# A three-stage decoder layer on one core: scatters ahead of GpSimd's splits, the last turn's sum in thirds, the tile map in four parts, and a tail shared between three engines

## The chip, the core and the metric

The kernel runs on one core of a Trainium2 chip. The time is the device time of one execution in microseconds, as the median of several runs. Five engines each work through their own queue in order: TensorE (PE), VectorE (DVE), ScalarE (ACT), GpSimd (POOL) and SyncE (SP, which here only issues DMAs). They wait for each other through semaphores.

## The reference

The input is 16 sequences of 56 tokens with 128 features, and for each sequence a context of 1500 rows with 96 features.

```
x = layernorm(x + mixer(x))                       # causal convolution, cumulative sums, gate
x = layernorm(x + attention(x, ctx))              # q = x Wq, k and v from the context, softmax over 1500
logits = x Wr + br; top two of 8 experts; w = softmax(top two)
o_e    = relu(x W1_e + b1_e) W2_e + b2_e          # 128 -> 512 -> 128
f = layernorm(x + sum over the two chosen experts of w_e o_e) * gamma + beta
x = layernorm(x + f)
```

## The kernel before

Two sequences make a pair of 112 rows, so there are eight pairs (0 to 7). The program has four stages.

1. The mixer, for two halves of the batch (0 to 75 us of the trace).
2. The attention loop. `attend_turn(i)` overlaps pairs: TensorE makes the scores of pair i+1, the context sum of pair i-1 and the transposes of pair i's weights in three thirds (`turn_weights`). VectorE finds the maximum of 1500 scores, copies two thirds of the transposed weights, and makes norms. ScalarE does the exponentials and the last third. `last_turn()` ends the loop for pairs 6 and 7.
3. The experts. Pairs 0 to 6 are routed: each row's two experts are found (`logits`, `top_two`, `select`), the row gets a slot in its expert's region (`ranks` on TensorE, `place` on VectorE), and GpSimd's indirect DMA `scatter(i, w)` writes it to HBM tensor `slots`; there are 14 such scatters. TensorE then works through a sequence of 28 items: five dense passes of pair 7 (all its rows through experts 0 to 4), 20 tiles of 128 routed rows, and three more dense passes. Item n is `hidden(n)` (16 matmuls) and `outs(n)` (13); ScalarE and VectorE split the hidden values into a high and a low half between them (`hidden_high`, `hidden_low`). Tiles 0 to 7 are the first tile of each expert; which experts own the other 12 is the tile map, found by 12 small VectorE operations on row totals. `turn_tile(t)` transposes a loaded tile; it waits for the load, and SyncE issues the loads only once all 14 scatters have landed (`r_scat`).
4. The tail. SyncE loads the two expert outputs of each row (`got`), TensorE adds them to x2 in PSUM for two pairs at a time (four quarters), and two layer norms follow before the store.

The order on each engine is the order of the code, written by hand. GpSimd's code is one list that mixes four jobs: `split_low` (half of an expert's weights, 128x512, which TensorE wants only in stage 3), `low_rows` and `second_weights` (which finish a row before its scatter), `plus_beta` (x2 + beta, wanted only in the tail) and `scatter`. `pause(k)` is a small memset that spaces scatters. The semaphores that matter are `r_slot` (slots found), `r_wt` and `r_row` (row complete), `a_et`, `a_et2` (transposed weights read), `r_map` (tile map found), `t_ld` (tile loaded), `f_y` (sums ready), `f_rstd`, `f_rstd2` (inverse deviations).

The lines that the prediction's steps touch:

```
1366 maximum       1416 slot_c in place    1433-1452 tile_map      1470 turned_copy (VectorE)
1750 scatter       1734 split_low          1730 plus_beta          931 turned_copy (ScalarE)
543 scores  553 turn_weights  566 context_sum  765-767 hidden  780-784 outs  744 turn_tile
806 summed (tail)  1668-1691 the two norms' moments  893-895 inverse deviation  1123 final_norm
```

## Time and profile before

| | |
|---|---|
| median of 3 runs | 206.45 us (205.98 to 206.97) |
| the profiled execution's own time | 205.7 us |
| its span in the trace | 203.9 us (1.8 us lie around it) |
| busy: TensorE matmul, VectorE, ScalarE, GpSimd | 173.8, 154.4, 117.6, 61.7 us |
| mean granted TensorE clock | 0.97 |

The trace lists instructions with their start, length and engine, and in brackets the idle time in front of an instruction and who ended it. The shares of busy time are means over stages: between 144 and 182 us TensorE is never idle, in the last 17 us it works for 3.9 us. "x48" on a TensorE row counts matmul records; an fp32 matmul leaves two.

### The profile page before, as it was taken

How to read it: one execution, taken by the hardware profiler on the slowest of the kernel's cores; microseconds unless marked ns; L12 is line 12 of the kernel's file. 1: busy time of each engine (PE TensorE's matmuls, PEld its weight loads, DVE VectorE, ACT ScalarE, POOL GpSimd, SP SyncE). 2: the span in 40 equal slices, each digit the busy share in tenths (PEclk: the TensorE clock that was granted, in tenths of full speed). 3: DMA queues.
4: the chain of work that ended last, by engine and by line, in shares of the span. 5: the costliest groups of instructions: out<-in, count | busy, mean ns of one | idle time of the engine just before them, and what ended most of it. 6: DMA issues, size and time to landing. Idle time of an engine off the chain costs nothing.

```text
span 203.9 us, 4768 instructions
## 1 busy us (share of the span) xinstructions
PE 173.8 (85%) x1721; PEld 127.5 (63%) x1721; DVE 154.4 (76%) x394; ACT 117.6 (58%) x246; POOL 61.7 (30%) x82
## 2 busy tenths in 40 slices
PE   7999999969799978799799998785999999996400
PEld 6554556644353664564656787584999999994300
DVE  1659999988979668558967885677688888743890
ACT  2189979722664515697676954442566777650544
POOL 4000000000040000029697568881045655550000
PEclk9999999999999999999999999997899999999965
DMA  6999999993899278779856911104234100005011
GB/s 133 335 212 294 229 296 259 407 412 140 217 351 323 81 253 208 270 187 309 208 200 189 345 47 36 35 25 106 57 83 104 40 22 26 19 0 161 2 45 45
DMA packets 13467, 34.20 MB, mean 168 GB/s; under 512 B 2096, under 2 KB 5606, under 8 KB 13443
## 3 DMA queue, kind: packets, MB, share of 16 engines
q1 hardware_dynamic: 12356, 32.27, 53.0%
q0 software_dynamic: 1088, 1.62, 2.6%
q8 instruction: 14, 0.23, 0.5%
q14 instruction: 9, 0.07, 0.1%
HBM read 28.01 MB, written 6.38 MB: 169 GB/s over the span
## 4 chain that ended last, share of the span: by engine, by line
PE 53%; DVE 20%; issue 10%; POOL 8%; ACT 4%; DMA 2%; POOLq 0%; ACTq 0%; DVEq 0%; SPq 0%
PE bank L490 9%; POOL ret L1832 8%; PE bank L543 8%; PE bank L566 6%; PE bank L509 5%; PE bank L500 5%; PE bank L553 5%; PE bank L478 4%; DVE neg_max L1366 2%; PE bank L767 2%; PE bank L784 2%; DVE ph L1470 2%; DMA ctxT_slot<-ret 1%; DVE xtok L1684 1%; PE bank L806 1%
## 5 line engine op out<-in xcount | busy, mean ns | idle before, releaser
L1084 ACT ACTIVATE ctx_slot<-bank 128x512 f16<-128x512 f32 (+1 forms) x28 | 16.3, 582 | 18.8 <-PE bank L767 18.7
L1832 POOL DMA_INDIRECT ret<-ctx_slot,ctxT_slot x20 | 19.7, 986 | 24.5 <-ACT ctx_slot L1097 20.8
L1598 DVE SCALAR_TENSOR_TENSOR ctx_slot<-bank,ctx_slot 128x512 f16<-128x512 f32 (+1 forms) x28 | 18.8, 671 | 9.6 <-ACT ctx_slot L1084 7.2
L543 PE MATMUL bank<-ctxT_slot,w_conv 97*64 97x500 f32 x96 | 21.8, 589 | 2.4 <-ACT pc L926 1.4
L1754 POOL TENSOR_TENSOR home<-home 128x896 f32<-128x896 f32 x1 | 2.1, 2077 | 55.3 <-ACT home L882 55.3
L490 PE MATMUL bank<-xpad,w_conv 128*128 128x448 f32 x48 | 18.5, 544 | 0.0
L784 PE MATMUL bank<-home,ctx_slot 128*112 128x128 f16 (+1 forms) x192 | 14.7, 227 | 3.2 <-DVE ctx_slot L1598 3.2
L1366 DVE TENSOR_REDUCE neg_max<-bank 120x1 f32<-120x1500 f32 x8 | 13.7, 1714 | 4.5 <-PE bank L543 4.5
L1734 POOL TENSOR_TENSOR home<-w_raw,home 128x512 f16<-128x512 f32 x10 | 11.5, 1164 | 14.8 <-DVE neg_max L1366 14.8
L1242 DVE TENSOR_TENSOR_SCAN home<-reset,home 128x896 f32<-128x896 f32 x8 | 15.8, 2008 | 0.0
L566 PE MATMUL bank<-ctx_slot,ph 125*64 125x96 f32 x336 | 15.4, 248 | 0.0
L784 PEld LDWEIGHTS bank<-home,ctx_slot 128*112 128x112 f16 (+1 forms) x192 | 12.6, 121 | 3.7 <-DVE ctx_slot L1598 3.5
L490 PEld LDWEIGHTS bank<-xpad,w_conv 128*128 128x128 f32 x48 | 9.1, 193 | 9.2 <-issue 8.7
L1750 POOL DMA_INDIRECT slots<-mix,slot_i x14 | 13.5, 963 | 4.6 <-issue 3.7
L566 PEld LDWEIGHTS bank<-ctx_slot,ph 125*64 125x64 f32 x336 | 14.1, 133 | 1.2 <-issue 0.7
L478 PE MATMUL bank<-reset 128*128 128x224 f32 x48 | 13.4, 424 | 1.4 <-DVE reset L1145 1.4
L543 PEld LDWEIGHTS bank<-ctxT_slot,w_conv 97*64 97x64 f32 x96 | 6.2, 133 | 13.0 <-issue 10.9
L765 PE MATMUL bank<-half_sb,b_hl 128*128 128x112 f16 (+1 forms) x64 | 13.8, 221 | 0.3 <-DVE turned_late L1561 0.3
L500 PE MATMUL bank<-home,w_blk 128*128 128x448 f32 x32 | 12.9, 545 | 0.0
L478 PEld LDWEIGHTS bank<-reset 128*128 128x128 f32 x48 | 10.7, 235 | 2.9 <-DVE reset L1145 1.4
L893 ACT ACTIVATE lnv<-mv,cst 112x2 f32<-112x2 f32 (+3 forms) x11 | 3.2, 293 | 15.6 <-DVE mv L1307 6.3
L767 PE MATMUL bank<-ctx_slot 128*128 128x128 f16 x144 | 12.0, 219 | 0.0
(223 smaller groups left out, 433.5 us busy)
## 6 DMA issues: line engine op xcount, KB each, us to landing
ctx_slot<-ctx SPq DMA_DIRECT2D x16, 576.0 KB, 5.7
ctxT_slot<-ctx_T SPq DMA_DIRECT2D x16, 562.5 KB, 9.5
w_raw<-w SPq DMA_DIRECT2D x16, 256.0 KB, 6.9
slots<-w_raw SPq DMA_DIRECT2D x4, 910.0 KB, 26.1
ctxT_slot<-slots SPq DMA_DIRECT2D x20, 65.0 KB, 1.9
convw_sb<-conv_w SPq DMA_DIRECT2D x3, 256.0 KB, 5.6
ctxT_slot<-ret SPq DMA_DIRECT2D x3, 224.0 KB, 3.1
small_sb<-small SPq DMA_DIRECT2D x1, 526.0 KB, 9.3
```

The lines of the kernel that those rows point to most:

```text
L478: mm = pe.matmul(bank[:, to, 0:HW // 2], reset[:, 0:D], reset[:, 0:HW // 2], start=True, stop=True)
L490: mm = pe.matmul(bank[:, Z[c, g], 0:HW], w_conv[:, g, k, :], xpad[:, HB * c:HB * (c + 1), k:k + L], start=(k == 0), stop=(k == TAPS - 1))
L500: mm = pe.matmul(bank[:, Y_BANK[c], 0:HW], w_blk[:, j, :], terms[:, j * HW:(j + 1) * HW], start=(j == 0), stop=(j == 2 * M - 1))
L543: mm = pe.matmul(bank[j * GAP:j * GAP + rows, n, 0:SN], qk_all[:, at:at + rows], ctxT_slot[:, s, j, n * SN:(n + 1) * SN], start=True, stop ...
L566: mm = pe.matmul(bank[j * GAP:j * GAP + rows, SUM_BANKS[i], 0:DC], expT_sb[i][:, c, j * GAP:j * GAP + rows], ctx_slot[0:KP, s, j, c, :], s ...
L767: mm = pe.matmul(to, w[:, 0, part, at], x[:, half, 0:cols], start=False, stop=(m == 2))
L784: mm = pe.matmul(to, h_[:, n % 3, f, 0:cols], w[:, 1, part, f * D:(f + 1) * D], start=False, stop=(h_ is hl and f == FC - 1))
L1084: nc.scalar.activation(hh[:, n % 3, :, 0:cols], bank[:, n % 3, :].rearrange("p (f t) -> p f t", f=FC) [:, :, 0:cols], ACT.Relu).then_inc(t ...
L1242: return V.tensor_tensor_scan(sums[:, w], reset[:, 0:W2], terms[:, w], 0.0, ALU.mult, ALU.add)
L1366: V.tensor_reduce(neg_max[0:GT, :], bank[0:GT, 0:SB, 0:SN], AX.XY, ALU.max, negate=True).then_inc(a_max, 1)
L1598: V.scalar_tensor_tensor(hl[:, n % 3, :, 0:cols], bank[:, n % 3, :].rearrange("p (f t) -> p f t", f=FC) [:, :, 0:cols], 0.0, hh[:, n % 3, ...
L1832: G.indirect_dma_start(ret[:], bass.IndirectOffsetOnAxis(ap=xs_u[:, t, D + 1:D + 2], axis=0), out_st[:, t % OB, :], None, bounds_check=2 * ...
```

## The change

- GpSimd: each `scatter` stands in front of the splits and of `plus_beta`; two of the six pauses go; the last three `plus_beta` move behind the scatters of output tiles 2, 3 and 4.
- The last turn: all three thirds of pair 7's weights are transposed before pair 6's context sum, pair 7's own sum is cut in three parts instead of two, and VectorE's and ScalarE's steps are put in another order. `ranks(4)` goes ahead of the first dense pass.
- Stage 3's start: pair 7's logits are read before its first low half; the tile map's 12 operations are spread over four places (`read_counts`, `count_extras`, `expert_of_tile`, `tile_map`); TensorE's first tile waits for `r_tot` (counts read) instead of `r_map`. The reads of the map into VectorE's registers begin four items later.
- The tail: pair 7, which needs nothing from the returned outputs, is normalised first, alone. For the others VectorE only centres and multiplies by gamma; ScalarE scales (`scaled`), TensorE adds x2 + beta in PSUM (`with_x2`), and the last norm is ScalarE's for quarters 0 and 1 and VectorE's for the rest. There are five stores instead of four.

The diff, cut to its core:

```diff
@@ tensor, turn_weights: @@
+                if third == 2 and i == PAIRS - 1:
+                    pe.wait_ge(a_et2, i)
@@ tensor, last_turn @@
                 turn_weights(q, 0)
                 turn_weights(q, 1)
+                turn_weights(q, 2)
                 context_sum(p)
                 turn_x2(p - 1)
                 ranks(2)
-                turn_weights(q, 2)
-                context_sum(q, range(0, KC // 2))
+                context_sum(q, range(0, KC // 3))
                 turn_sum(p)
                 logits(p - 1)
-                context_sum(q, range(KC // 2, KC))
+                context_sum(q, range(KC // 3, 2 * KC // 3))
                 values(p)
+                context_sum(q, range(2 * KC // 3, KC))
@@ tensor, turn_tile and the start of stage 3 @@
-                    pe.wait_ge(r_map, 1)
+                    pe.wait_ge(r_tot, 1)
...
+            ranks(4)
             hidden(0)
-            ranks(4)
+            logits(PAIRS - 1)
             totals()
...
-                if n == 0:
-                    logits(PAIRS - 1)
@@ tensor, tail @@
+            def returns(q):
+                w = slice(2 * q, min(2 * q + 2, XP))
+                added(SUM_AT[q], x2[:, w, :], start=True)
+                pe.wait_ge(g_ld[q], 16)
+                added(SUM_AT[q], got[:, w, 0, :])
+                added(SUM_AT[q], got[:, w, 1, :], stop=True).then_inc(f_y, 1)
+
+            def with_x2(q):
+                w = slice(2 * q, min(2 * q + 2, XP))
+                added(NORM_AT[q], x2b[:, w, :], start=True)
+                pe.wait_ge(f_scaled, q + 1)
+                added(NORM_AT[q], acc[:, w, :], stop=True).then_inc(f_sum, 1)
...
+            returns(0)
+            returns(1)
+            returns(2)
+            with_x2(0)
+            returns(3)
+            with_x2(1)
+            with_x2(2)
+            with_x2(3)
@@ scalar, end of the loop @@
+            turned_copy(PAIRS - 1)
             route_weights(2)
             high_rows(PAIRS - 3)
-            turned_copy(PAIRS - 1)
+            split_high(1, POOL_SPLITS - 1)
             turned_sum(PAIRS - 2)
             route_weights(3)
+            attended_inv_std(PAIRS - 2)
             turned_sum(PAIRS - 1)
-            attended_inv_std(PAIRS - 2)
+            high_rows(PAIRS - 2)
             attended_inv_std(PAIRS - 1)
-            high_rows(PAIRS - 2)
@@ scalar, tail @@
+            def scaled(q):
+                act.wait_ge(f_cent, q + 1)
+                act.wait_ge(f_rstd, q + 2)
+                for j in range(2 * q, min(2 * q + 2, XP)):
+                    ins = nc.scalar.activation(acc[:, j, :], acc[:, j, :], ACT.Copy, scale=rstd[:, j:j + 1])
+                ins.then_inc(f_scaled, 1)
@@ vector, last_turn @@
                 turned_copy(q)
+                select(2)
                 sum_copy(p)
...
+                attended_stats(p)
+                sum_copy(q)
                 select(3)
-                sum_copy(q)
-                attended_stats(p)
+                attended_norm(p)
                 place(3)
-                attended_norm(p)
-                attended_stats(q)
-                x2T_copy(p)
+                attended_stats(q, between=lambda: x2T_copy(p))
                 logit_read(p, q)
                 attended_norm(q)
                 top_two(p, q)
+                select(4)
                 dve.wait_ge(t_x7h, 1)
...
-                select(4)
                 place(4)
@@ vector, tail @@
+            def returned(q):
                 dve.wait_ge(f_y, q + 1)
+                moments(q + 1, returned_at, f_var)
+                dve.wait_ge(f_var, q + 2)
+                for j in range(2 * q, min(2 * q + 2, XP)):
+                    ins = V.scalar_tensor_tensor(acc[:, j, :], returned_at(j), mv[:, j, 0:1], par("gamma", PT),
+                                                 ALU.subtract, ALU.mult)
+                ins.then_inc(f_cent, 1)
+            def summed(q):
+                dve.wait_ge(f_sum, q + 1)
+                moments(q + 1, normed_at, f_var2)
@@ gpsimd: tile outputs @@
+                if 2 <= t < 5:
+                    plus_beta(PAIRS - 5 + t)
```

The first place is GpSimd's queue in the attention loop, from the low halves of the first rows on, before the change (L1725 `low_rows`, L1741 `second_weights`, L1730 `plus_beta`, L1734 `split_low`, L1750 `scatter`):

```order
L1725 TENSOR_TENSOR mix<-rows_late,mix 112x2x128 x2
L1741 TENSOR_TENSOR mix<-mix,tsm 112x2
L1730 TENSOR_TENSOR rows_late<-rows_late,small_sb 112x128 x2
L1734 TENSOR_TENSOR home<-w_raw,home 128x512
L1750 DMA slots<-mix,slot_i 7296x130
L1734 TENSOR_TENSOR home<-w_raw,home 128x512
L1750 DMA slots<-mix,slot_i 7296x130
L1725 TENSOR_TENSOR mix<-rows_late,mix 112x2x128
L1750 DMA slots<-mix,slot_i 7296x130
```

and after it (L1793, L1809, L1798, L1802 and L1818 are the same five):

```order
L1793 TENSOR_TENSOR mix<-rows_late,mix 112x2x128 x2
L1809 TENSOR_TENSOR mix<-mix,tsm 112x2
L1818 DMA slots<-mix,slot_i 7296x130
L1798 TENSOR_TENSOR rows_late<-rows_late,small_sb 112x128 x2
L1818 DMA slots<-mix,slot_i 7296x130
L1802 TENSOR_TENSOR home<-w_raw,home 128x512
L1818 DMA slots<-mix,slot_i 7296x130
L1802 TENSOR_TENSOR home<-w_raw,home 128x512
```

The first scatter now stands in front of two `plus_beta` and of every further split; later scatters move up in the same way.

The second place is VectorE's queue at the start of stage 3, before (L1598 `hidden_low`, L1378 to L1396 pair 7's logits and choice, L1580 to L1584 its weights):

```order
L1598 SCALAR_TENSOR_TENSOR ctx_slot<-bank,ctx_slot 128x4x112
L1378 TENSOR_TENSOR logit<-bank,small_sb 112x8
L1386 MAX top<-logit 112x8
L1388 TENSOR_TENSOR tsm<-top 112x1
L1390 MAX_INDEX topi<-top,logit 112x8
L1396 TENSOR_TENSOR chosen<-small_sb,topi 112x16
L1580 TENSOR_SCALAR rw<-chosen,tsm 112x8
L1581 TENSOR_SCALAR rw<-chosen,tsm 112x8
L1584 TENSOR_TENSOR rw<-rw 112x8
L1598 SCALAR_TENSOR_TENSOR ctx_slot<-bank,ctx_slot 128x4x112
L1625 SCALAR_TENSOR_TENSOR xtok<-bank,rw,rows_late 112x128
L1430 TENSOR_SCALAR counts<-bank 1x8
```

and after (L1640 is `hidden_low`, L1465 `read_counts`, L1622 to L1626 the weights, L1667 `pair_out`):

```order
L1414 TENSOR_TENSOR logit<-bank,small_sb 112x8
L1422 MAX top<-logit 112x8
L1424 TENSOR_TENSOR tsm<-top 112x1
L1426 MAX_INDEX topi<-top,logit 112x8
L1640 SCALAR_TENSOR_TENSOR ctx_slot<-bank,ctx_slot 128x4x112
L1432 TENSOR_TENSOR chosen<-small_sb,topi 112x16
L1465 TENSOR_SCALAR counts<-bank 1x8
L1622 TENSOR_SCALAR rw<-chosen,tsm 112x8
L1623 TENSOR_SCALAR rw<-chosen,tsm 112x8
L1626 TENSOR_TENSOR rw<-rw 112x8
L1640 SCALAR_TENSOR_TENSOR ctx_slot<-bank,ctx_slot 128x4x112
L1667 SCALAR_TENSOR_TENSOR xtok<-bank,rw,rows_late 112x128
```

Pair 7's logits stand in front of the first `hidden_low`, and of the tile map only one operation (L1465) is left before the second one. Before, all 12 followed pair 7's first output (L1625) in one run.

The third place is ScalarE's queue in the tail before, from its first instruction there (L893 and L895 an inverse deviation, L1123 a final norm):

```order
L893 ACTIVATE lnv<-mv,cst 112x2
L895 ACTIVATE rstd<-lnv 112x2
L893 ACTIVATE lnv<-mv,cst 112x2
L895 ACTIVATE rstd<-lnv 112x2
L893 ACTIVATE lnv<-mv,cst 112x2
L895 ACTIVATE rstd<-lnv 112x2
L893 ACTIVATE lnv<-mv,cst 112x2
L895 ACTIVATE rstd<-lnv 112x2
L1123 ACTIVATE x<-xtok,nmr,rstd 112x128 x2
L893 ACTIVATE lnv<-mv,cst 112x2
L895 ACTIVATE rstd<-lnv 112x2
```

and after, from the first inverse deviation of a quarter on (L916, L918; L1149 `scaled`, L1155 the final norm):

```order
L916 ACTIVATE lnv<-mv,cst 112x2
L918 ACTIVATE rstd<-lnv 112x2
L1149 ACTIVATE xtok<-xtok,rstd 112x128 x2
L916 ACTIVATE lnv<-mv,cst 112x2
L918 ACTIVATE rstd<-lnv 112x2
L1149 ACTIVATE xtok<-xtok,rstd 112x128 x2
L916 ACTIVATE lnv<-mv,cst 112x2
L918 ACTIVATE rstd<-lnv 112x2
L916 ACTIVATE lnv<-mv,cst 112x2
L918 ACTIVATE rstd<-lnv 112x2
L1149 ACTIVATE xtok<-xtok,rstd 112x128 x2
```

Between the inverse deviations ScalarE now also scales, and it reads its final norm from PSUM.

## Rows read from the trace of the kernel before

**Rows 1.** Part 4 of the page: the chain that ended last, by engine

```profile
PE 53%; DVE 20%; issue 10%; POOL 8%; ACT 4%; DMA 2%; POOLq 0%; ACTq 0%; DVEq 0%; SPq 0%
```

**Rows 2.** Busy time by stretch; its columns are in its first line

```profile
core 0: us, PE busy (x) PEld busy (x) DVE busy (x) ACT busy (x) POOL busy (x), PEclk, DMA share, GB/s
...
131.00:144.00 13.00, 9.76 (x150) 9.44 (x151) 8.99 (x35) 5.29 (x12) 6.33 (x11) 0.87 0.26 62
144.00:182.00 38.00, 38.00 (x686) 37.91 (x686) 29.88 (x62) 24.90 (x58) 19.25 (x20) 1.00 0.17 45
```

**Rows 3.** Timeline of VectorE, place(0) and place(1): start, length, engine, line, operation, idle

```profile
98.92 1.89 DVE L1416 TENSOR_TENSOR slot_c<-chosen,slot_e 112x32 f32<-112x32 f32 x1
...
115.12 0.20 DVE L1416 TENSOR_TENSOR slot_c<-chosen,slot_e 112x32 f32<-112x32 f32 x1
```

**Rows 4.** Timeline of GpSimd at the first scatter

```profile
98.87 0.77 POOL L1730 TENSOR_TENSOR rows_late<-rows_late,small_sb 112x128 f32<-112x128 f32 x2
99.60 1.16 POOL L1734 TENSOR_TENSOR home<-w_raw,home 128x512 f16<-128x512 f32 x1
102.06 1.12 POOL L1750 DMA_INDIRECT slots<-mix,slot_i  x1 [1.30 <-issue]
```

**Rows 5.** Timeline of TensorE, transposes of pairs 4 and 5

```profile
99.44 1.13 PE L553 MATMUL bank<-small_sb,pc 120*125 120x120 f32 x8
...
101.87 0.70 PE L553 MATMUL bank<-small_sb,pc 120*125 120x120 f32 x4 [0.16 <-DVE ph L1470]
...
107.86 1.13 PE L553 MATMUL bank<-small_sb,convw_sb 120*125 120x120 f32 x8
...
109.30 0.70 PE L553 MATMUL bank<-small_sb,convw_sb 120*125 120x120 f32 x4 [0.21 <-DVE ph L1470]
```

**Rows 6.** Timeline of GpSimd from the last splits to the last scatter

```profile
115.73 2.28 POOL L1734 TENSOR_TENSOR home<-w_raw,home 128x512 f16<-128x512 f32 x2
...
120.52 0.95 POOL L1750 DMA_INDIRECT slots<-mix,slot_i  x1 [0.15 <-POOL mix L1725]
...
136.16 0.95 POOL L1750 DMA_INDIRECT slots<-mix,slot_i  x1 [0.17 <-issue]
```

**Rows 7.** Timeline of SyncE's queue, loads of the first eight tiles

```profile
138.50 3.65 SPq L453 DMA_DIRECT2D ctxT_slot<-slots  x8
```

**Rows 8.** Part 6 of the page: count, KB each, median us from issue to landing

```profile
ctxT_slot<-slots SPq DMA_DIRECT2D x20, 65.0 KB, 1.9
```

**Rows 9.** Timeline of TensorE, its waits in the last turn and stage 3's start

```profile
122.65 1.21 PE L566 MATMUL bank<-ctx_slot,home 125*64 125x96 f32 x24 [0.65 <-ACT home L931]
...
136.41 0.43 PE L784 MATMUL bank<-home,ctx_slot 128*112 128x128 f16 x4 [0.83 <-DVE ctx_slot L1598]
...
140.54 0.68 PE L784 MATMUL bank<-home,ctx_slot 128*112 128x128 f16 x4 [2.41 <-DVE ctx_slot L1598]
```

**Rows 10.** Timeline of VectorE: x7's low half, pair 6's slots, tile map

```profile
130.53 0.27 DVE L1561 TENSOR_TENSOR turned_late<-bank,turned_late 128x112 f16<-128x112 f32 x1 [0.33 <-ACT turned_late L1074]
...
132.66 0.17 DVE L1419 TENSOR_REDUCE slot_i<-slot_c 112x2 int32<-112x16 f32 x1
...
137.33 0.61 DVE L1435 TENSOR_SCALAR counts<-counts 1x8 f32<-1x8 f32 x1
```

**Rows 11.** Timeline of the tail, VectorE and ScalarE

```profile
188.51 0.30 ACT L893 ACTIVATE lnv<-mv,cst 112x2 f32<-112x2 f32 x1 [5.30 <-DVE mv L1671]
...
190.95 0.49 DVE L1688 BATCH_NORM_STATS2 stat<-xtok 112x6 f32<-112x128 f32 x2
...
193.69 0.49 DVE L1688 BATCH_NORM_STATS2 stat<-xtok 112x6 f32<-112x128 f32 x2
...
200.01 0.28 ACT L893 ACTIVATE lnv<-mv,cst 112x2 f32<-112x2 f32 x1
...
200.32 0.20 ACT L895 ACTIVATE rstd<-lnv 112x2 f32<-112x2 f32 x1
...
200.75 0.88 ACT L1123 ACTIVATE x<-xtok,nmr,rstd 112x128 f32<-112x128 f32 x2 [0.23 <-DVE nmr L1698]
```

More of the change, by code:

```diff
@@ L464, in _ @@
                 sp_.dma_start(got[:, w], ret.rearrange("(p i w) d -> p i w d", p=PT, i=XP)[:, w]).then_inc(g_ld[q], 16)
-            for q in range(4):
-                sp_.wait_ge(f_out, q + 1)
-                w = slice(2 * q, 2 * q + 2)
+            for n, w in enumerate((slice(XP, PAIRS), slice(0, 2), slice(2, 4), slice(4, 6), slice(6, XP))):
+                if n in (1, 2):
+                    sp_.wait_ge(f_out, n)
+                else:
+                    sp_.wait_ge(f_outv, n - 1 if n else 1)
                 sp_.dma_start(out[:, w, :], x1[:, w, :]).then_inc(s_store, 16)
-            sp_.wait_ge(s_store, 16 * 4)
+            sp_.wait_ge(s_store, 16 * 5)
         @block.tensor
@@ L1479, in attended_stats @@
                 a = loop.mark(V.bn_stats(attend_stat[:, s], res[:, s]))
+                if between:
+                    between()
                 loop.need(a)
@@ L1643, in _ @@
                     pair_out(n)
-                if n == 0:
-                    tile_map()
+                if n == 1:
+                    scanned = count_extras()
+                if n == 2:
+                    summed_tiles = expert_of_tile(scanned)
+                if n == 3:
+                    tile_map(summed_tiles)
                 if 4 <= n < 10:
                     split_low(n % 2, POOL_SPLITS + (n - 4) // 2)
-                for k in range(n - 1, n) if 1 <= n <= EXTRA else ():
-                    expert_of_extra(k)
+                if 5 <= n < 5 + EXTRA:
+                    expert_of_extra(n - 5)
                 if n == HEAD + E - 3:
@@ L1653, in _, with moments @@
                     staged(n - (HEAD + E - 3))
-            def summed_at(j):
-                if j == XP:
-                    return acc[:, j, :]
-                return bank[0:PT, (3, 7, 0, 1)[j // 2], (j % 2) * D:(j % 2 + 1) * D]
+            def moments(n, at, done):
+                pairs = range(XP, PAIRS) if n == 0 else range(2 * n - 2, min(2 * n, XP))
+                for j in pairs:
+                    a = own.mark(V.bn_stats(stat[:, j, :], at(j)))
+                own.need(a)
+                for j in pairs:
+                    a = V.bn_aggr(mv[:, j, :], stat[:, j, :])
+                a.then_inc(done, 1)
@@ L1694, in final_bias, with vector_final @@
             def final_bias(q):
                 w = slice(2 * q, 2 * q + 2)
-                dve.wait_ge(f_rstd2, q + 1)
+                dve.wait_ge(f_rstd2, q + 2)
                 V.scalar_tensor_tensor(nmr[:, w], mv[:, w, 0], -1.0, rstd2[:, w], ALU.mult, ALU.mult).then_inc(f_bias, 1)
+            def vector_final(n):
+                dve.wait_ge(f_rstd2, n + 1)
+                for j in range(XP, PAIRS) if n == 0 else range(2 * n - 2, min(2 * n, XP)):
+                    ins = V.tensor_scalar(x1[:, j, :], normed_at(j) if n else acc[:, j, :], mv[:, j, 0:1],
+                                          rstd2[:, j:j + 1], ALU.subtract, ALU.mult)
+                ins.then_inc(f_outv, 1)
@@ L1799, in _ @@
             second_weights(1)
+            scatter(2, 0)
             plus_beta(3)
+            scatter(2, 1)
             split_low(0, 4)
+            scatter(3, 0)
+            low_rows(4)
+            plus_beta(4)
+            scatter(3, 1)
             split_low(1, 4)
-            low_rows(4)
-            scatter(2, 0)
-            plus_beta(4)
-            scatter(2, 1)
-            pause(0)
-            scatter(3, 0)
-            low_rows(5)
-            scatter(3, 1)
-            second_weights(2)
-            pause(1)
-            scatter(4, 0)
-            pause(2)
+            second_weights(2)
+            scatter(4, 0)
+            low_rows(5)
             scatter(4, 1)
             second_weights(3)
-            pause(3)
+            pause(0)
             scatter(5, 0)
+            pause(1)
+            scatter(5, 1)
             low_rows(6)
-            scatter(5, 1)
             second_weights(4)
-            pause(4)
             scatter(6, 0)
-            pause(5)
+            pause(2)
             scatter(6, 1)
-            for i in range(PAIRS - 3, PAIRS):
-                plus_beta(i)
             for t in range(TILES):
```

158 lines of the change are left out of this document (78 added, 80 removed).

## The prediction, made before the changed kernel ran

> **What bounds the kernel now.** I read the chain of waits first. It lies on TensorE for 53% and on VectorE for 20%, GpSimd having 8% [rows 1]; so a gain must come from TensorE's gaps or from a stage where it has little to do. The table by stretch shows which: from 144 to 182 us TensorE is busy 38.0 of 38.0 us at a granted clock of 1.00, while from 131 to 144 us it is busy for 9.8 of 13 us and the mean clock is 0.87 [rows 2]. Nothing in this change shortens the 38 us. What it can shorten is the attention loop where TensorE waits, the 13 us after it, and the tail. For these I read the timelines of the engines.
>
> **The loop (pair 4's turn).** VectorE's slot_c operation lasts 1.89 us, where the same form takes 0.20 us one group later [rows 3]. It starts at 98.92 and ends at 100.81; GpSimd is in two plus_beta and then in a split until 100.76 [rows 4]. VectorE's copies of the transposed weights queue behind it, and TensorE gets to its last third 2.43 us after its first (101.87 - 99.44), against 1.44 us a turn later [rows 5]. The difference is 0.99 us. After the change the scatter stands ahead of plus_beta and of the split, and the scatter waits for the slots; so GpSimd reads nothing while slot_c runs. Gain 1.0 us. Bounds: up to 1.2, and down to -0.5 if the two splits, moved some 3 us, fall on the norm of that turn instead.
>
> The Trainium skill (SBUF — State Buffer, "Who interferes with whom") says that a VectorE instruction with two SBUF inputs contends with a GpSimd instruction that reads SBUF, and that the later one fully blocks. By that rule the trace agrees: 1.89 us against 0.20, ending 0.05 us after the split.
>
> **The last turn.** Pair 7's last third is transposed before pair 6's context sum, so the 0.65 us in which TensorE waited for ScalarE's copy is covered by 2.1 us of sum [rows 9]. The new wait on a_et2 is for a copy of pair 6 that is over before it; behind it in the queue is only that sum. Part is given back, since pair 7's norm still hangs on VectorE and ScalarE in turn, and select(4) now stands in front of x7's low half (two operations, 0.4 us). I follow the queues and get x7's low half 0.4 us earlier than 130.53 [rows 10]. ranks(4), 0.3 us, lies before hidden(0) in a wait instead of behind it.
>
> **From the last turn to the first tile.** TensorE reaches the first tile's transposes 0.47 us into the row at 140.54, at 141.0. On the way it waits 0.83 and 2.41 us [rows 9]. The second is VectorE in 12 small tile-map operations, each waiting for the one before (one is 0.61 us for eight numbers [rows 10], while GpSimd runs its last three plus_beta); pair 2's low half stands behind them. In four parts, no part is longer than about 0.9 us, less than the 1.5 us of one item, and the low halves come in time. The last moment at which TensorE would be ready is then 141.0 - 0.83 - 2.41 - 0.4 - 0.3 - 0.3 (half-clock part of the last outs, and pair 7's waits) = 136.8 at the latest, 136.4 by the sum of its items.
>
> But the tile has to be there. Ten scatters take 136.16 - 120.52 = 15.6 us, 1.74 us each [rows 6]. GpSimd is late with them: it does two splits from 115.73 [rows 6], although pairs 2 and 3 had slots one short operation after the slot_c that ends at 115.32 [rows 3]; and pair 6's slots are ready at 132.83 [rows 10] while the last two scatters start at 134.67 and 136.16. Now the scatters of pair 2 start at 115.6; nine spacings of 1.74 and the two splits put between (2.3 us) give 133.6. Pair 6's slots come some 1.5 us earlier (0.4 from the turn, and ranks(4) is no longer behind 0.8 us of hidden(0) and its queue), at 131.3; from there 0.2, 1.5 and nothing else give 133.0. I take 133.2, 3.0 us earlier than 136.16. The loads of the tiles were issued at 138.50 [rows 7], 2.3 us behind the last scatter; now 135.5. A load lands after 1.9 us [rows 8]: 137.4. So the first tile starts at 137.4 and no longer at 141.0; TensorE waits there 0.6 to 1.0 us for data in place of 3.2 us for VectorE. That is 3.6; I take 3.4 us, since this long walk forgets hand-offs. Bounds: 0.6 us, if the last scatter does not move (138.50 + 1.9 = 140.4), and 4.2 us, if data never hold TensorE.
>
> **The clock.** 13 us at a mean of 0.87 [rows 2] miss 13 x 0.13 = 1.7 us of full clock: half clock (1.2 GHz instead of 2.4) for some 3.4 us. It falls in the wait of 2.41 us, the four matmuls behind it take 0.68 us, while after the wait of 0.83 us the same four take 0.43 [rows 9]. With a longest wait of about 1 us the level of 2.4 GHz holds. 0.2 us of it is counted above: gain 1.4 us. Bounds 0 and 1.5.
>
> **The tile stage.** Three plus_beta now lie among the scatters of tile outputs, and four more map reads on VectorE beside the staged copies. VectorE is busy for 29.9 of the 38.0 us [rows 2], so it has some 0.4 us to spare per tile of 1.73 us, and a two-input operation that meets a plus_beta (0.4 us) loses it. I take -0.4 us, bounds 0 and -1.6 (four tiles late by 0.4).
>
> **The tail.** VectorE sets it: the same step recurs after 2.74 us (190.95, 193.69), and ScalarE ends last at 200.75 + 0.88 = 201.6 [rows 11]. Pair 7 goes into the wait for the returned outputs, some six short operations on VectorE where ScalarE's own wait is 5.30 us long [rows 11]. For the others VectorE keeps per quarter the moments twice and one multiplication, about 2.0 us, 8.8 us with the last norms, so it would be through at 196.5. ScalarE becomes the bound. From 188.5 on it has 8 inverse deviations at 0.51 (0.31 to the second instruction and 0.20) and 11 activations at 0.44 (0.88 for two) [rows 11]: 4.1 + 4.8 = 8.9 us, so 197.4, with hand-offs 197.8. Behind it stand VectorE's last two norms, 0.9 us: 198.7, 2.9 us before 201.6. The stores now come three in 1.5 us from one queue; I give 0.4 us back. Gain 2.5 us, bounds 1.0 (TensorE's added sums at half clock and each in the chain) and 3.2.
>
> **The sum** is against the profiled execution itself, 205.7 us (span 203.9 and 1.8 around it): 1.0 + 3.4 + 1.4 - 0.4 + 2.5 = 7.9, so 197.8. The median of the runs, 206.45, lies 0.75 above that execution; on its scale the forecast is 198.5 us.
>
> **Rivals.**
> - The clock falls all the same. TensorE's wait for the first tile lies between the 0.83 us that did no harm and the 2.41 us that did. If it does, the 1.4 us stay: 199.9. For it: the pause in the middle may come on top of the short ones around it. Chance 0.18.
> - The scatters don't come earlier. Their gate is pair 6's choice, and row 120.52 only says that GpSimd was late early on; if the last one is 1.5 us later than I think, tile and clock suffer: 1.5 + 0.5, 200.5. Chance 0.14, of which 0.04 for the following. A scatter that starts while VectorE is in a copy could be held up. Against it: the one at 102.06 ran beside copies of pair 4 and took 1.12 us instead of 0.95 [rows 4, 6]. The Trainium skill (SBUF — State Buffer, "SBUF: two separate sides") has this as a trap: during a VectorE operation that uses both ports, GpSimd cannot write the descriptors of its DMA. By that rule scatters moved into VectorE's busy turns would lose what they gain.
> - The tail gives nothing, because hand-offs among three engines replace one queue: each quarter goes VectorE, ScalarE, TensorE, VectorE, ScalarE, VectorE. Then 201.0. Against it: four quarters are in flight at a time. Chance 0.10.
> - Almost everything fails together: within 0.5% of before. Chance 0.04.
> - Slower. The tile stage passes from TensorE to VectorE: hidden_low, a staged copy of 2048 columns and now a map read per tile stand in one queue, and with GpSimd's plus_beta each tile could take 2.2 us in place of 1.73. The other terms bring 8.3 us over 20 tiles, so it decides from 0.42 us per tile on; at 0.47 (9.4 us) it gives 1.1 us above before, 207.5. Against it: the map reads stood beside such copies for three tiles before, and the 38 us show no gap [rows 2]. Chance 0.04.
>
> **Numbers.** The forecast has 0.50. Its own range is 197.3 to 199.6. The range for 8 in 10 takes in the clock, the late scatters and most of a lost tail: 196.5 to 202.0; its lower end is 2.0 us under the forecast, about what data that never hold TensorE (0.8), a better tail (0.7) and no loss in the tile stage (0.4) would give. About 0.5% is what a measurement of this kernel can tell from no change. Faster by more than that: 0.50 + 0.18 + 0.14 + 0.10 = 0.92, same 0.04, slower 0.04.
>
> **What the profile after would show.** slot_c of the first group at 0.2 us, and 1.4 us between TensorE's two groups of transposes in that turn. The last scatter about 4 us earlier on the clock of the trace (1.0 of it from the loop), the first tile loads 2.3 us behind it, TensorE's wait in front of the first tile ended by that load and about 1 us long, no granted clock under 0.97 between 130 and 143. 28 items without a gap from there. In the tail ScalarE busiest, its queue over about 2.9 us sooner after the first sum. I am wrong if the first tile's wait is over 2 us, if the tile stage shows gaps, or if VectorE is still the last in the tail.

## The result and the profile after

Median of 4 runs: 200.17 us (198.75 to 201.02), against 206.21 us (205.93 to 206.97) of the kernel before on the same chip; ratio 0.971, 95% interval 0.967 to 0.975. The profiled execution took 200.14 us with a span of 198.3 us: 5.6 us less than the 203.9 us before, where the forecast had 7.9. Medians here and below are over all executions of a kernel, while ratios and their intervals leave out executions more than 1.5% above the kernel's fastest.

The busy time by stretch shows where the forecast missed. These are rows of the changed kernel; after the stretch stand its length, then TensorE, its weight loads, VectorE, ScalarE, GpSimd, the granted clock, the DMA share and GB/s.

```profile
125.00:130.00 5.00, 3.46 (x19) 2.76 (x19) 3.81 (x20) 1.90 (x8) 4.09 (x8) 0.71 0.12 35
130.00:137.40 7.40, 7.40 (x79) 7.26 (x78) 3.96 (x18) 2.56 (x8) 3.74 (x6) 0.50 0.10 27
137.40:142.00 4.60, 4.40 (x83) 4.25 (x81) 3.51 (x13) 3.19 (x6) 0.00 (x0) 1.00 0.52 118
142.00:180.00 38.00, 38.00 (x686) 37.79 (x684) 31.13 (x67) 24.87 (x57) 22.06 (x23) 1.00 0.17 45
```

From 130 to 137.4 us TensorE never waits, but it is granted 0.50: 1.2 instead of 2.4 GHz. Before, the granted clock fell only at 140.5 us and was back by 144 [rows 2, 9]. The 38 us of tiles are full as they were [rows 2]; one gap of 0.20 us lies just before them, at 141.55 us.

The timeline of TensorE says what it did as the clock fell (start, length, engine, line, operation, idle time in front and who ended it):

```profile
98.86 1.13 PE L560 MATMUL bank<-small_sb,pc 120*125 120x120 f32 x8
100.30 0.70 PE L560 MATMUL bank<-small_sb,pc 120*125 120x120 f32 x4 [0.21 <-DVE ph L1515]
...
121.16 0.34 PE L616 MATMUL bank<-sel,half_sb 112*112 112x8 f16 x4 [0.54 <-DVE sel L1441]
...
125.34 0.32 PE L585 MATMUL bank<-small_sb,u_sb 120*97 120x120 f32 x1 [0.59 <-DVE u_sb L1509]
126.24 0.39 PE L616 MATMUL bank<-sel,half_sb 112*112 112x8 f16 x5 [0.58 <-DVE sel L1441]
...
127.45 0.98 PE L483 MATMUL bank<-reset 128*128 128x224 f32 x2
...
139.64 0.28 PE L752 MATMUL bank<-half_sb,ctxT_slot 128*128 128x128 f16 x2
```

Pair 4's two groups of transposes are 1.44 us apart, as forecast [rows 5]. The granted clock is 1.00 until 127.1 us and 0.50 from there. Behind the waits at 125.3 and 126.2 the pair of matmuls of L483 at 127.45, which takes 0.56 us at full clock, takes 0.98. The first tile's transposes (139.64) wait for nothing: at half clock TensorE comes later than the data.

GpSimd and VectorE meet elsewhere now. GpSimd's rows, then VectorE's:

```profile
102.84 1.16 POOL L1802 TENSOR_TENSOR home<-w_raw,home 128x512 f16<-128x512 f32 x1
...
122.12 1.16 POOL L1802 TENSOR_TENSOR home<-w_raw,home 128x512 f16<-128x512 f32 x1
...
132.54 0.94 POOL L1818 DMA_INDIRECT slots<-mix,slot_i  x1 [1.04 <-DVE slot_i L1455]
...
134.02 0.95 POOL L1818 DMA_INDIRECT slots<-mix,slot_i  x1 [0.17 <-issue]
```

```profile
98.34 0.19 DVE L1452 TENSOR_TENSOR slot_c<-chosen,slot_e 112x32 f32<-112x32 f32 x1
...
102.75 1.35 DVE L1536 TENSOR_SCALAR rows_late<-res,attend_mv,attend_rstd 112x128 f32<-112x128 f32 x1 [0.55 <-ACT attend_rstd L918]
...
121.79 1.53 DVE L1452 TENSOR_TENSOR slot_c<-chosen,slot_e 112x16 f32<-112x16 f32 x1
...
130.02 0.27 DVE L1607 TENSOR_TENSOR turned_late<-bank,turned_late 128x112 f16<-128x112 f32 x1
...
131.49 0.17 DVE L1455 TENSOR_REDUCE slot_i<-slot_c 112x2 int32<-112x16 f32 x1
...
140.49 0.24 DVE L1480 TENSOR_TENSOR ge<-counts,small_sb 1x96 f32<-1x96 f32 x1
...
141.38 0.27 DVE L1632 COPY ctx_slot<-bank 128x256 f16<-128x256 f16 x1
```

The slot_c that took 1.89 us [rows 3] takes 0.19. But the norm at 102.75 lasts 1.35 us (0.34 where nothing meets it) and ends with the split, and pair 5's slot_c at 121.79 lasts 1.53 us and also ends with a split. Pair 6's slots are ready at 131.66; the first of the last two scatters starts 0.9 us later. The last scatter starts at 134.02, 2.1 us before 136.16 [rows 6]; SyncE issues the tile loads 2.3 us behind it, as before [rows 7]:

```profile
136.35 3.65 SPq L456 DMA_DIRECT2D ctxT_slot<-slots  x8
```

The tail, on TensorE, ScalarE and VectorE:

```profile
191.91 0.69 PE L812 MATMUL bank<-xtok,small_sb 112*112 112x256 f32 x2 [0.95 <-ACT xtok L1149]
```

```profile
191.17 0.69 ACT L1149 ACTIVATE xtok<-xtok,rstd 112x128 f32<-112x128 f32 x2
191.77 0.79 ACT L1155 ACTIVATE x<-bank,nmr,rstd 112x128 f32<-112x128 f32 x2
...
193.79 0.79 ACT L1155 ACTIVATE x<-bank,nmr,rstd 112x128 f32<-112x128 f32 x2
```

```profile
195.04 1.05 DVE L1762 TENSOR_SCALAR x<-bank,mv,rstd 112x128 f32<-112x128 f32 x3
```

TensorE and VectorE wait for ScalarE here, whose queue has no gap over 0.15 us from 189.9 to 194.5. It is not the busiest engine, though: from 182.5 to 196.1 us it is busy for 8.52 us and VectorE for 10.37. The last norm ends at 196.09, where the last one before ended at 201.63 [rows 11].

### The profile page after: what moved, and what is told of

It is laid out like the page before. It is cut to its first block, busy times and chain, and to the rows that moved or that the text cites. A ratio compares the mean times of both kernels' runs of the same rounds, so it can differ in the third digit from the quotient of the medians.

```text
span 198.3 us, 4799 instructions
## 1 busy us (share of the span) xinstructions
PE 178.5 (90%) x1737; PEld 131.4 (66%) x1737; DVE 154.9 (78%) x389; ACT 119.2 (60%) x253; POOL 62.0 (31%) x79
## 4 chain that ended last, share of the span: by engine, by line
PE 54%; DVE 16%; issue 9%; POOL 9%; DMA 5%; ACT 4%; SPq 0%; POOLq 0%; DVEq 0%; ACTq 0%
PE bank L495 9%; POOL ret L1893 8%; PE bank L548 7%; PE bank L514 5%; PE bank L505 5%; PE bank L573 5%; PE bank L560 4%; PE bank L775 3%; PE bank L483 3%; PE bank L792 2%; DMA convw_sb<-conv_w 2%; DMA ctxT_slot<-ret 2%; DVE rows_late L1536 2%; DVE neg_max L1402 2%; PE bank L812 2%
## 5 line engine op out<-in xcount | busy, mean ns | idle before, releaser
L1893 POOL DMA_INDIRECT ret<-ctx_slot,ctxT_slot x20 | 20.2, 1009 | 22.9 <-ACT ctx_slot L1122 16.4
L1640 DVE SCALAR_TENSOR_TENSOR ctx_slot<-bank,ctx_slot 128x512 f16<-128x512 f32 (+1 forms) x28 | 18.8, 671 | 9.0 <-ACT ctx_slot L1109 7.6
L1818 POOL DMA_INDIRECT slots<-mix,slot_i x14 | 13.4, 960 | 9.2 <-DVE slot_i L1455 5.2
L1802 POOL TENSOR_TENSOR home<-w_raw,home 128x512 f16<-128x512 f32 x10 | 11.4, 1160 | 14.9 <-DVE neg_max L1402 14.8
L773 PE MATMUL bank<-half_sb,b_hl 128*128 128x112 f16 (+1 forms) x64 | 14.6, 231 | 0.2 <-issue 0.2
L483 PE MATMUL bank<-reset 128*128 128x224 f32 x48 | 13.0, 413 | 1.4 <-DVE reset L1181 1.4
L792 PE MATMUL bank<-home,ctx_slot 128*112 128x128 f16 (+1 forms) x192 | 14.1, 225 | 0.0
L483 PEld LDWEIGHTS bank<-reset 128*128 128x128 f32 x48 | 10.3, 228 | 2.9 <-DVE reset L1181 1.4
L514 PE MATMUL bank<-home,small_sb 128*128 128x448 f32 x28 | 11.0, 545 | 0.0
```

The lines of the kernel that those rows point to most:

```text
L483: mm = pe.matmul(bank[:, to, 0:HW // 2], reset[:, 0:D], reset[:, 0:HW // 2], start=True, stop=True)
L514: mm = pe.matmul(bank[:, SS_BANK[c], 0:HW], par("group_mask"), sums[:, j * HW:(j + 1) * HW], start=(j == 0), stop=(j == 2 * M - 1))
L792: mm = pe.matmul(to, h_[:, n % 3, f, 0:cols], w[:, 1, part, f * D:(f + 1) * D], start=False, stop=(h_ is hl and f == FC - 1))
L1640: V.scalar_tensor_tensor(hl[:, n % 3, :, 0:cols], bank[:, n % 3, :].rearrange("p (f t) -> p f t", f=FC) [:, :, 0:cols], 0.0, hh[:, n % 3, ...
L1893: G.indirect_dma_start(ret[:], bass.IndirectOffsetOnAxis(ap=xs_u[:, t, D + 1:D + 2], axis=0), out_st[:, t % OB, :], None, bounds_check=2 * ...
```

## The experiments

One reading serves them all: the profiled executions start pair 3's transposes, which nothing in the change touches, anywhere from 90.2 to 91.5 us. The table is counted from that row; "last scatter" and "first tile" (its transposes) are starts, worked out from the timelines. Pair 3's row and pair 5's, first before, then after:

```profile
91.06 1.13 PE L553 MATMUL bank<-small_sb,convw_sb 120*125 120x120 f32 x8
...
107.86 1.13 PE L553 MATMUL bank<-small_sb,convw_sb 120*125 120x120 f32 x8
```

```profile
90.48 1.13 PE L560 MATMUL bank<-small_sb,convw_sb 120*125 120x120 f32 x8
...
106.53 1.13 PE L560 MATMUL bank<-small_sb,convw_sb 120*125 120x120 f32 x8
```

The last column is the time at half clock between 125 and 145 us, worked out as twice the share missing from the granted clock in the stretches of 5 us.

| profiled execution | last scatter | first tile | from there to the end of the last outs | from there to the span's end | at half clock, us |
|---|---|---|---|---|---|
| before | 45.10 | 49.95 | 43.35 | 19.5 | 3.4, from 140.5 |
| after | 43.54 | 49.16 | 42.44 | 16.2 | 10.3, from 127.1 |
| after_again | 43.48 | 48.57 | 42.44 | 17.9 | 6.8 |
| map_whole | 43.52 | 49.15 | 42.07 | 16.6 | 6.9 |
| warm_again | 43.49 | 47.64 | 42.10 | 17.6 | 3.4 |
| warm_more | 43.45 | 47.70 | 42.09 | 19.4 | 0 |
| two_parts | 44.54 | 49.90 | 42.07 | 16.1 | 6.9 |
| scatters_again | 43.47 | 48.00 | 42.08 | 20.1 | 0 |
| tail_again | 45.22 | 51.33 | 41.94 | 18.0 | 10.2 |
| filled | 43.47 | 49.02 | 42.07 | 17.6 | 6.8 |

My first theory was that the new last turn made the clock fall; the rival, that it falls whatever the order. The first four kernels ran on a chip on which the kernel before took 212.12 us (211.23 to 213.12) and TensorE showed gaps among the tiles (busy 18.8 of the 20 us from 160 to 180 in scatters_only; from the first tile to the last outs 48.7 to 49.1 us where the table has 42 to 43). The changed kernel was not measured on that chip. So these four are read by their ratios to the kernel before, and two of them stand below once more on another chip.

**tail_only**: the kernel before with the new tail.

```diff
+            returns(0)
+            returns(1)
+            returns(2)
+            with_x2(0)
+            returns(3)
...
+            scaled(0)
...
+            vector_final(3)
```

> The kernel before with the new tail alone (pair 7 first, ScalarE's scaling, TensorE's adding, five stores). Theory: the tail is worth what the two traces show between the first landed return and the last norm, 15.1 us before and 12.05 us after, so 3.0 us: 203.2 us. Rival: the tail's gain is the 2.5 us of the prediction and the rest came from elsewhere: 203.7 us. Rival that hand-offs eat it: 206 us.

209.04 us, 3.1 us less than before on this chip, ratio 0.982 (0.975 to 0.990): near the theory's 3.0, though the interval doesn't exclude the 2.5. Its program up to the tail is the one before, yet in this execution the clock fell in the last turn:

```profile
125.00:130.00 5.00, 3.14 (x24) 2.06 (x20) 3.59 (x20) 2.11 (x10) 4.17 (x8) 0.94 0.08 23
130.00:135.00 5.00, 4.49 (x42) 3.80 (x43) 2.57 (x14) 1.76 (x6) 3.06 (x5) 0.50 0.14 38
```

So the new last turn isn't needed for it.

**scatters_only**: GpSimd's order alone. With it go three of the six pauses (the list of changes says two; the changed kernel keeps three) and a move of ScalarE's `route_weights` for the first two groups by one place.

```diff
+            scatter(0, 0)
             plus_beta(0)
             plus_beta(1)
+            scatter(0, 1)
             split_low(0, 2)
```

> The kernel before with GpSimd's new order alone. Theory: pair 4's turn gains 1.0 us, of which the splits moved onto the norm and the second group's slots take back 0.3 to 0.4 us; the last scatter comes earlier, but the tile map in one piece still holds TensorE and its clock still falls: 205.4 us. Rival (the prediction): 1.0 us from the loop stays whole: 205.2 us, and with GpSimd out of the tile map's way 204.7 us. Rival: contention only moves, 206.2 us.

207.34 us, ratio 0.977 (0.972 to 0.982): 4.8 us, more than I had given it, on this chip.

**old_turn**: the changed kernel with the old last turn on three engines.

```diff
-                turn_weights(q, 2)
                 context_sum(p)
                 turn_x2(p - 1)
                 ranks(2)
+                turn_weights(q, 2)
+                context_sum(q, range(0, KC // 2))
```

> The changed kernel with the last turn of before (thirds, VectorE's and ScalarE's order), all else new. Theory (the clock fell in the new last turn, at 126.8 us): the granted clock holds through 130 to 137 us as it did before, the first tile starts when its data land: 1.7 us less than the changed kernel, 198.5 us. Rival (the new order of the last turn is worth its 0.4 us, and the clock fell by something else): 200.6 us, with the clock still at half between 130 and 137 us.

205.42 us, ratio 0.963 (0.956 to 0.969). The clock fell here too (0.78 from 125 to 130 us, 0.50 to 135). The first theory is down. This kernel keeps `ranks(4)` ahead of the first dense pass, and its last scatter is at 44.84, counted as in the table.

**warm**: two fillings, each one matmul without use, in TensorE's waits at 125.3 and 126.2 us.

```diff
                 context_sum(q, range(2 * KC // 3, KC))
+                keep_warm(1, 4)
                 turn_sum(q)
+                keep_warm(1, 4)
                 ranks(3)
```

> The changed kernel with two more matmuls without use (0.55 us each) in TensorE's waits before pair 7's sum is turned and before the fourth ranks. Theory (TensorE's waits between 120.6 and 126.2 us made the clock fall): granted clock 1.00 from 125 to 137 us, hidden(0) at 0.20 and 0.31 us per group as before, first tile transposes held only by its load (138.3 us): 198.5 us. Rival (the clock is not what costs, the order of the work or the data is): 200.2 us or 0.2 more, with the clock whole. Rival (the clock falls all the same, since small matmuls and not gaps are the reason): 200.4 us with the clock at half.

205.10 us, ratio 0.964 (0.956 to 0.972), no better than old_turn. In its profile the clock stayed at 1.00 from 120 to 188 us and the first tile came at 47.57, waiting 0.90 us for its load; but that one execution took 210.76 us, so nothing about the time follows from it. On the next chip (before: 206.39 us) the changed kernel stands beside it.

**after_again**: no edit.

> The changed kernel itself, for its spread on one chip beside the others. Theory now (the stretch from 120 to 130 us is so thin for TensorE, in the kernel before too, that its clock falls there in some executions and holds in others): the runs part in two groups, mean clock about 0.97 and about 0.985, the latter 1.5 us shorter; median 0.971 of before. Rival (the new last turn always makes it fall): all runs at 0.967 to 0.979 and no second group.

200.19 us (198.48 to 202.52), ratio 0.967 (0.963 to 0.972), mean clocks from 0.962 to 0.995. The spread is wider than the clock's two groups: 198.48 us came at 0.980, 198.89 at 0.995. In its profile the clock fell a second time, in the tail (0.58 from 184 to 188 us), and the tail took 17.9 us instead of 16.2.

**warm_again**: as warm.

> The changed kernel with the two added matmuls without use, once more. Theory (waits make the clock fall): mean clock of most runs about 0.985, median 1.0 to 1.7 us under the changed kernel's on the same chip. Rival (they don't decide it, or the time is bound by the tiles' loads anyway): within 0.5 us of the changed kernel.

201.04 us (198.91 to 203.38), ratio 0.972 (0.967 to 0.977): no gain, though four of six executions have a mean clock of 0.981 to 0.988. The profile shows both halves. The clock falls later and for 3.4 us only, the first tile comes 0.9 to 1.5 us earlier (table) and waits for its load; at the other end the time is gone again:

```profile
137.89 0.28 PE L754 MATMUL bank<-half_sb,ctxT_slot 128*128 128x128 f16 x2 [0.17 <-DMA ctxT_slot<-slots]
...
183.66 1.12 PE L814 MATMUL bank<-ctxT_slot,small_sb 112*112 112x256 f32 x4 [2.53 <-DMA ctxT_slot<-ret]
```

```profile
177.14 0.97 POOL L1895 DMA_INDIRECT ret<-ctx_slot,ctxT_slot  x1 [0.54 <-issue]
```

```profile
180.90 1.74 SPq L467 DMA_DIRECT2D ctxT_slot<-ret  x4
```

SyncE loads the returned outputs once the last of them has landed: 3.76 us behind the start of that scatter (of tile outputs), where all ten profiles of kernels without added matmuls have 2.18 or 2.19. The four with them have 3.60 to 3.76. Beside it one more row differs. The page lists a queue of instruction loads. In the half microsecond that follows the last scatter's issue, warm_again moves some 16 KB (33 GB/s for 0.5 us); in the changed kernel the same stands 2.0 us behind the scatter's start, about when it lands:

```profile
178.14:178.64 0.50, 0.50 (x13) 0.50 (x11) 0.10 (x1) 0.34 (x1) 0.00 (x0) 1.00 0.17 33
```

```profile
181.23:181.73 0.50, 0.50 (x9) 0.35 (x7) 0.50 (x2) 0.00 (x0) 0.00 (x0) 1.00 0.12 33
```

In the traces' DMA records a 16 KB packet of an instruction queue starts 1.3 to 1.5 us behind that scatter's start in the four profiles with added matmuls, and 2.1 us or more behind it in the other ten. That a load which comes before the landing holds it up by 1.5 us is my reading; it is not shown, since no run moved the load alone.

**map_whole**: the tile map in one piece again.

```diff
-                if n == 1:
-                    scanned = count_extras()
-                if n == 2:
-                    summed_tiles = expert_of_tile(scanned)
-                if n == 3:
-                    tile_map(summed_tiles)
+                if n == 0:
+                    tile_map()
...
-                    pe.wait_ge(r_tot, 1)
+                    pe.wait_ge(r_map, 1)
```

> The changed kernel with the tile map in one piece again (12 operations behind the first item, TensorE's first tile waiting for all of them). Theory from the trace of the kernel with GpSimd's order alone (its map took 2.3 us, since no plus_beta of GpSimd's lay beside it, TensorE waited 1.35 us, and the first tile's data landed no earlier): 0 to 0.4 us slower than the changed kernel. Rival (the prediction: the map in one piece is the wait of 2.4 us and takes the clock down with it): 2 us slower.

199.54 us (198.47 to 200.14), ratio 0.966 (0.963 to 0.970); the changed kernel beside it had 200.19. The four parts bring nothing that can be measured. At equal time at half clock they bring the first tile 0.6 us earlier (48.57 against 49.15, a wait of 0.46 us), and the tiles then take 0.37 us more (table). The 0.37 us lie in front of the second tile (the gap at 141.55): there four operations of the map, from 140.49 on, stand ahead of VectorE's copy at 141.38. With four parts but a first tile held by its load (warm_again, warm_more) the tiles take 42.10 and 42.09.

```profile
139.35 0.43 PE L792 MATMUL bank<-home,ctx_slot 128*112 128x128 f16 x4 [0.46 <-DVE ctx_slot L1631]
```

**two_parts**: the kernel before with GpSimd's order and the new tail, that is, the changed kernel without the rest:

```diff
-                turn_weights(q, 2)
                 context_sum(p)
...
-            ranks(4)
             hidden(0)
+            ranks(4)
...
+                if n == 0:
+                    tile_map()
```

> The kernel before with GpSimd's order and the new tail, without the other two parts (the last turn and stage 3's start are the old ones, the map in one piece). Theory: these two parts carry the whole gain, ratio to before 0.970, 200.2 us where before is 206.4. Rival (the prediction: the last turn in thirds and the map in four parts are worth 1 us or more): 201.3 us or more.

200.13 us (198.37 to 202.22), ratio 0.971 (0.964 to 0.978), before 206.03: the whole gain, from two of the four parts, as far as an interval of 1.4 us to either side can tell. The ratios of its two parts alone (0.986 and 0.987 below) multiply to 0.973.

**scatters_again**: as scatters_only, on the same chip as two_parts.

> The kernel before with GpSimd's order alone, once more beside the rest. Theory: loop 0.7 us, first tile and the clock behind it 2.3 us, 3.0 us together: 203.4 us where before is 206.4. Rival (what an earlier chip showed, ratio 0.977): 201.7 us. Rival (the prediction's 1.0 + 0.7): 204.7 us.

203.28 us, ratio 0.986 (0.978 to 0.993): 2.8 us, near the theory's 3.0; the interval takes in the 1.7 us of the second rival and ends just short of the ratio of 0.977 of the first. Its map shows what the wait of 2.41 us [rows 9] was made of:

```profile
136.37 0.16 DVE L1433 TENSOR_SCALAR counts<-counts 1x8 f32<-1x8 f32 x1
136.56 0.16 DVE L1435 TENSOR_SCALAR counts<-counts 1x8 f32<-1x8 f32 x1
...
138.41 0.16 DVE L1452 TENSOR_SCALAR map_r<-mapf 1x12 int32<-1x12 f32 x1
```

```profile
139.15 0.43 PE L784 MATMUL bank<-home,ctx_slot 128*112 128x128 f16 x4 [1.36 <-DVE ctx_slot L1598]
```

With plus_beta gone the two operations of about 0.6 us (one of them in [rows 10]) take 0.16, the wait is 1.36 us, and the clock holds through it.

**tail_again**: as tail_only.

> The kernel before with the new tail alone, once more beside the rest. Theory: 3.0 us, 203.4 us where before is 206.4. Rival (the prediction): 2.5 us, 203.9 us.

202.85 us, ratio 0.987 (0.981 to 0.993): 3.2 us, and again 3.0 and 2.5 are both inside. In its profile the clock fell in the tail too:

```profile
184.00:188.00 4.00, 2.66 (x9) 1.38 (x9) 2.62 (x12) 1.03 (x5) 0.00 (x0) 0.87 0.70 199
188.00:192.00 4.00, 4.00 (x13) 3.15 (x14) 2.19 (x9) 2.12 (x8) 0.00 (x0) 0.71 0.06 16
```

The tail then takes 18.0 us instead of 16.1 (two_parts), as in after_again (17.9): the new tail has given TensorE twice the matmuls in the chain.

**warm_more**: warm with two more fillings.

```diff
                 turn_x2(p - 1)
+                keep_warm(1, 4)
                 ranks(2)
...
                 logits(p)
+                keep_warm(1, 4)
                 turn_x2(q)
```

> The changed kernel with four added matmuls without use (0.56 us each), two more than the kernel with two: also in the waits before the third ranks and before pair 7's x2 is turned. Theory (waits make the clock fall and two fillings were too few): mean clock 0.985 or more in most runs; of the time at most 1 us, since the first tile then waits for its load: 199.2 us where the changed kernel has 200.2. Rival (the time between runs is spread by something else than the clock): clock up, time 200.2 us with the same spread of 4 us.

202.02 us (201.24 to 204.58), ratio 0.982 (0.976 to 0.989), the slowest version of the whole change, at mean clocks of 0.98 and more in four of six executions. At a whole clock the first tile is no earlier than in warm_again (47.70 and 47.64): TensorE waits there for data, so the clock no longer sets that point:

```profile
139.23 0.29 PE L756 MATMUL bank<-half_sb,ctxT_slot 128*128 128x128 f16 x2 [1.66 <-DMA ctxT_slot<-slots]
```

**filled**: map_whole with warm's two fillings and two in the tail.

```diff
                 added(SUM_AT[q], x2[:, w, :], start=True)
+                if q == 0:
+                    keep_warm(2, SUM_AT[1])
                 pe.wait_ge(g_ld[q], 16)
```

> The changed kernel with the tile map in one piece, the two added matmuls without use in the last turn, and two more (1.1 us) in TensorE's wait for the first returned outputs. Theory (in the tail TensorE now has twice the work in the chain, and its clock falls there too in some executions, after that wait of 0.8 to 2.5 us, which costs 1 to 1.9 us): granted clock 1.00 from 180 to 192 us, every run at or under 200 us where before is 206.2, median 198.7 (ratio 0.964), mean clock 0.985 or more. Rival (the fall in the tail is not decided by that wait): clock and spread as before the filling, 198.5 to 202.5 us, median 200.2. Rival (the filling delays the first sum): 200.8 us with the clock whole.

201.25 us (199.50 to 203.61), ratio 0.977 (0.972 to 0.982). The clock held in the tail (1.00 from 180 to 192 us) and fell in the last turn despite the fillings. The theory is 2.5 us off in time. The fillings delayed no sum (TensorE still waited 1.61 us for the load behind them), so the third rival falls too; the last scatter landed late, as in warm_again. No version is measurably faster than two_parts or the changed kernel (map_whole's ratio of 0.966 is within the noise of their 0.971 and 0.967).

## Why the prediction was right, and where it was not

The time came out 1.7 us over the forecast, inside the range but outside the forecast's own 197.3 to 199.6. It was the width kept for the rivals that took it in: two of them happened, the clock (199.9) and the late scatters (200.5), and a better tail paid for part. Profile to profile, 5.6 us are 0.6 (an earlier start of pair 3, which the change doesn't touch), 0.8 up to the first tile, 0.9 among the tiles and 3.3 in the tail. The forecast had 4.4, 1.0 and 2.5 for the last three. That it ended inside the range is in part luck.

- **Loop, 1.0.** Mechanism right: slot_c 0.19 us. From pair 3's transposes to pair 5's is 16.80 us before and 16.05 after: 0.75. It is 16.80 in all three profiles with GpSimd's old order and 16.03 to 16.05 in all eleven with the new one. The rest is the bound that I had named, a split on that turn's norm (1.35 us instead of 0.34). The Trainium skill (SBUF — State Buffer, "Who interferes with whom") counts tensor_scalar among the operations that can take the port pair shared with GpSimd; the norm is one, and the trace agrees: it ends 0.10 us behind the split. By the records the norm starts 0.09 us before the split and is held all the same.
- **Last turn and first tile, 3.4.** This step failed. The last scatter was to come 4.0 us earlier with the loop's 1.0. Counted from pair 3 it comes 1.6 us earlier (45.10 to 43.54), 0.8 beyond the loop, which leaves it 2.4 us later than forecast. Two terms of the walk make 1.7 of that.
  - x7's low half was to come 0.4 us earlier than the loop alone gives. It is 39.54 us behind pair 3's row, and before it was 39.47. With the old last turn and GpSimd's new order it is at 38.78 (scatters_again) and 38.92 (two_parts), and in the six profiles of the table with the new turn at 39.38 to 39.54. So the new turn puts it 0.6 us later: it brings pair 6's norm forward by 0.4 us (35.9 to 35.5) and pair 7's back by 0.5 (37.8 to 38.3). `ranks(4)` in its new place gives that back: from x7's low half to pair 6's slots are 1.47 us instead of 2.15 (0.7, where 1.1 was counted). At a whole clock the slots come at 40.9 with either turn (warm_more, scatters_again), and so does the last scatter, at 43.5.
  - From pair 6's slots to the next scatter I had put 0.2 us. It is 0.9 (131.66 to 132.54).

  The contention that the moved splits make (slot_c at 121.79 loses 1.3 us) is not the reason: scatters_again has it too (1.60 us), and its x7 is 0.69 us earlier than before, about what the loop gained. What the new turn, together with `ranks(4)`, does buy is cover when the clock falls: then the old turn has its last scatter at 44.54 (two_parts) and 44.84 (old_turn, where `ranks(4)` is in its new place), the new one stays at 43.5.
- **Clock, 1.4.** Half right. Behind the first tile the gain came: the tiles take 42.07 us with the map in one piece, 43.35 before. But the clock fell earlier instead. I looked only at the longest wait, and wrote "no granted clock under 0.97 between 130 and 143". It fell at 127.1 us, in the stretch in which both kernels are thin (TensorE busy 3.5 of 5 us). It fell there or just behind in seven of the ten profiles of the table, with the old last turn and the new. Up to 3.4 us at half clock cost nothing at the first tile, since data hold it anyway; 6.8 to 10.3 us cost 0.9 to 1.5 us with the new last turn (47.7 against 48.6 to 49.2) and 1.9 with the old (48.0 against 49.9). So of the 3.6 us that are missing up to the first tile, 2.1 are missing at a whole clock too, and 1.5 are the clock. The forecast's own rival had the size (199.9) but another place. The Trainium skill (TensorE: Matmul & The Clock Gate, Part 1) says that the stretch which the chip looks at runs free of the kernel, so that one program comes out differently from run to run. The traces agree as to the outcome: up to the tail one program held its clock in the last turn in one execution (before, scatters_again) and lost it there in another (tail_again, two_parts). That this is the reason no run shows.
- **Map in four parts.** I had the right wait and the wrong cure: 2.41 us came down to 1.36 by plus_beta moving away, and data are late anyway.
- **Tile stage, -0.4.** The size was luck. plus_beta and the later map reads among the tiles, which I had counted, stand in map_whole as well, at 42.07 us; tail_again, with GpSimd's old order, has 41.94. That is 0.1 us. The other 0.37 (42.44) is the map's third part in front of one copy.
- **Tail, 2.5.** Mechanism right, ScalarE's queue sets the pace from 189.9 us on; the size was 3.3 (19.5 to 16.2). I had counted a scaled pair at 0.88 us, it takes 0.69, and 0.4 for the stores, which is not seen: from the last norm to the span's end are 2.2 us, before 2.3. Where the clock fell in the tail (after_again), 1.6 are left, which is the lower bound's case. One sign was badly chosen: "if VectorE is still the last in the tail" holds (195.04), but the sum itself had put VectorE's last two norms there. Nor is ScalarE busiest.

The rival in which scatters are held up by VectorE's copies did not happen: those in the turns take 0.94 to 0.96 us, the first 1.12 as before.

Open: what makes the clock hold or fall in the last turn, since with two fillings it fell not at all in one profile (warm), for 3.4 us in another and for 6.8 in a third; why pair 7's norm comes later in the new turn; what the late landing of the last scatter has to do with the instruction load; and the spread of about 4 us among executions of one program.

## What to carry to other kernels

When an operation is moved away from one that it blocks, look for what it blocks at its new place before counting the gain: here a quarter of the loop's gain went that way. When a gain rests on one event, follow the path to that event and give every hand-off the length that rows show: 0.4 us gained that was 0.6 lost, and 0.2 us that measured 0.9, were 1.7 of the 2.4 us by which the last scatter missed. Time an edit alone before keeping it: two of four parts carried the whole gain that could be measured. A stretch in which the granted clock falls in some executions of one program is a risk for all that stands behind it, and a price of 1 to 2 us should stand in the sum with a chance, not as a yes or no.

## What the runs showed of the hardware

- Two to four added matmuls went with a last scatter of tile outputs that landed 1.5 us later, some 50 us behind the place of the edit, in four of four profiles.
- Up to the tail one program ran at a whole clock in one execution (scatters_again) and at half clock for 6.9 us in another (two_parts), both on one chip.
- Operations of 0.2 and 0.34 us on VectorE took 1.53 and 1.35 us, each ending within 0.1 us of a GpSimd operation of 1.16 us.
- A wait of 2.53 us in the tail left the clock whole in warm_again and was followed by half clock in warm_more; a mean clock of 0.987 stood beside 199.42 and 200.82 us of one kernel.
- The kernel before had medians of 205.5 to 206.4 us in four comparisons and 212.1 us in one.
